# Moving the low halves of the layer norm from GpSimd to VectorE, and issuing the raw-row gathers in one run, in the start-up of a graph network kernel

## The reference

```python
# block 1: graph layer, one LSTM step, projection
xn  = (x - mean(x)) / sqrt(var(x) + 1e-5)            # by row
agg = segment_sum(xn[src], dst, num_segments=6250)
h   = relu(agg @ W_rel + b_rel + xn @ W_root)        # 256 -> 512
i, f, g, o = split(h @ W_ih.T + b_ih + b_hh, 4)      # 512 -> 2048
x   = x + (sigmoid(o) * tanh(sigmoid(i) * tanh(g))) @ W_fc + b_fc
# block 2: slice attention over all rows (8 heads, 64 slices) on layernorm(x)
x   = x + ffn(layernorm(x))
```

## Time and profile before

| what | value |
|---|---|
| median of three runs | 1594.67 us |
| range of the runs | 1590.57 to 1596.51 us |
| span of the profiled execution, first to last instruction | 1292.3 us |
| median less span (launch and end, not in the trace) | 302.4 us |
| busy share: TensorE, VectorE, ScalarE, GpSimd | 92%, 64%, 48%, 65% |
| chain that ended last: TensorE, ScalarE, VectorE | 80%, 10%, 4% |
| granted TensorE clock, mean | 0.995 of 2.4 GHz |

### The profile page before, as it was taken

One profiled execution on the slowest core, in us unless ns is written; L12 is line 12 of the kernel. 1 busy time (PEld: TensorE's weight loads), 2 busy tenths in 40 slices (PEclk: granted clock), 3 DMA queues, 4 the chain that ended last, 5 costly groups with the idle time before them and its releaser, 6 DMA issues.

```text
span 1292.3 us, 25492 instructions
## 1 busy us (share of the span) xinstructions
PE 1182.8 (92%) x8463; PEld 1052.9 (81%) x8463; DVE 830.3 (64%) x2412; ACT 622.6 (48%) x1248; POOL 844.0 (65%) x884
## 2 busy tenths in 40 slices
PE   0317999999999999999999999999999999999998
PEld 0315888898889888888888888888888888897798
DVE  7767375667566756676567656765676667546655
ACT  5662354545454445544554455444544453555332
POOL 4767777777777777777777777777777777600000
PEclk9998999999999999999999999999999999999999
DMA  8674445544554455444544454445544544423499
GB/s 300 206 260 113 121 114 146 143 139 115 144 145 138 123 136 144 137 124 131 144 138 131 127 145 139 135 121 147 142 130 122 146 143 130 114 67 96 124 330 285
DMA packets 122534, 191.82 MB, mean 148 GB/s; under 512 B 51451, under 2 KB 84193, under 8 KB 122457
## 3 DMA queue, kind: packets, MB, share of 16 engines
q0 software_dynamic: 41008, 111.77, 30.1%
q1 hardware_dynamic: 70894, 60.20, 15.8%
q10 hardware_dynamic: 10575, 19.20, 4.4%
HBM read 159.02 MB, written 32.92 MB: 149 GB/s over the span
## 4 chain that ended last, share of the span: by engine, by line
PE 80%; ACT 10%; issue 4%; DVE 4%; DMA 1%; POOL 1%; ACTq 0%; DVEq 0%; SPq 0%; POOLq 0%
PE ps L384 19%; PE ps L386 19%; PE ps L385 19%; PE ps L1039 13%; PE ps L1147 5%; ACT ps L820 3%; ACT L802 2%; ACT x L810 2%; PE ps L1135 2%; PE ps L1099 1%; PE ps L1073 1%; PE ps L1076 1%; ACT ring L753 1%; DVE stats L1346 1%; DMA table<-pick_room 1%
## 5 line engine op out<-in xcount | busy, mean ns | idle before, releaser
L675 POOL DMA_INDIRECT ring<-table,sidx x833 | 797.7, 958 | 258.0 <-issue 251.4
L384 PE MATMUL ps<-h_h,wih_h 128*128 128x256 f32 x1200 | 346.4, 289 | 4.1 <-DVE wxs_l L1666 4.1
L385 PE MATMUL ps<-h_l,wih_h 128*128 128x256 f32 x1200 | 339.8, 283 | 0.0
L386 PE MATMUL ps<-h_h,wih_l 128*128 128x256 f32 x1200 | 339.7, 283 | 0.0
L1039 PE MATMUL ps<-ring,oneh 128*125 128x512 f16 x974 | 229.6, 382 | 26.3 <-DVE oneh L1492 26.3
L384 PEld LDWEIGHTS ps<-h_h,wih_h 128*128 128x128 f32 x1200 | 230.2, 192 | 7.6 <-issue 4.5
L385 PEld LDWEIGHTS ps<-h_l,wih_h 128*128 128x128 f32 x1200 | 230.3, 192 | 1.7
L386 PEld LDWEIGHTS ps<-h_h,wih_l 128*128 128x128 f32 x1200 | 230.2, 192 | 0.0
L835 ACT ACTIVATE gate<-ps,bgate 128x256 f32<-128x256 f32 x300 | 125.8, 472 | 210.6 <-PE ps L386 210.6
L1039 PEld LDWEIGHTS ps<-ring,oneh 128*125 128x125 f16 x974 | 132.3, 138 | 91.8 <-DVE oneh L1492 26.5
L1492 DVE TENSOR_SCALAR oneh<-iota,rel 128x125 f16<-128x125 f16 x974 | 166.4, 286 | 1.8
(11 more groups left out here) (226 smaller groups left out, 2529.9 us busy)
## 6 DMA issues: line engine op xcount, KB each, us to landing
ring<-table,sidx POOLq DMA_INDIRECT x833, 2.7
swt_d<-swt ACTq DMA_DIRECT2D x25, 500.0 KB, 3.0
gate<-swt_d SPq DMA_DIRECT2D x19, 500.0 KB, 6.2
x_room<-in_x SPq DMA_DIRECT2D x12, 512.0 KB, 5.8
xn<-table SPq DMA_DIRECT2D x25, 224.0 KB
xin<-in_x SPq DMA_DIRECT2D x25, 224.0 KB
res<-xin SPq DMA_DIRECT2D x25, 224.0 KB
table<-tile_room SPq DMA_DIRECT2D x8, 512.0 KB, 5.5
```

What stands on the lines that cost most here:

```text
L384: eng.matmul(dst, wh, xh, start=first, stop=False)
L385: eng.matmul(dst, wh, xl, start=False, stop=False)
L386: return eng.matmul(dst, wl, xh, start=False, stop=last)
L675: pool.indirect_dma_start(ring[:, j, :], None, table, bass.IndirectOffsetOnAxis(ap=sidx[:, odd * SLOTS + j:odd * SLOTS + j + 1], axis=0)). ...
```

## The change

VectorE now does the low halves of all 13 chunks: in round k of its first pass, after the statistics of chunk k+2 and the planning step, it does that of chunk k-1. GpSimd does no low half any more. After the wait for the edge lists it issues `gather_x` 0 to 8, then waits for the plan's value and issues the planning gather, then `gather_x` 9 to 17.

```diff
             pool.wait_ge(idx_in[0], LIST)
-            for k in range(NCH - 1):
-                if k == 5:
+            for j in range(RAW):
+                if j == RAW // 2:
                     pool.wait_ge(plan_v, 3)
                     pool.indirect_dma_start(edge_i[0:NW + 1, 0:ER], None, a["dst"].rearrange("(p b) -> p b", b=ER),
                                             bass.IndirectOffsetOnAxis(ap=coli[0:NW + 1, 0:1], axis=0)).then_inc(ld_rows, 16)
-                ln_low(pool, k)
-                if k >= 5:
-                    gather_x(k - 5)
-            for j in range(NCH - 6, RAW):
                 gather_x(j)
             pool.wait_ge(plan_done, 2)
...
                 for n, step in ((2, plan_a), (3, plan_a2), (4, plan_a3), (5, plan_b), (9, bias_rows), (10, plan_c), (11, plan_c2)):
                     if k == n:
                         step()
-            ln_low(dve, NCH - 1)
+                if k:
+                    ln_low(dve, k - 1)
             ln_low(dve, NCH)
             plan_d()
```

## The result

The changed kernel takes 1568.91 us in the median of five runs (1566.51 to 1581.27). Five runs of the kernel before beside them have a median of 1594.67 us (1582.1 to 1596.51).

The account below looks back on a forecast made before the run. It took TensorE and GpSimd's gather stream as both full, the later one deciding: 7.7 us gained on TensorE's path, 6.8 on the stream. Against the median of 1594.67 us, the 6.8 gave 1587.9 us; range 1583.5 to 1595 us.

Parts of the forecast that it names:

- The 302.4 us around the span stay: Whole execution: 302.4 us of the time lie outside the profiled span of 1292.3 us and do not change.
- First pass: Start-up on VectorE: 12.7 us of added low halves, paid by waits and held-up instructions; last store 1.6 us earlier, at 55.5.
- the five held-up instructions: First pass on VectorE: five instructions lengthened beside GpSimd's low halves return to clean durations, giving back 7.7 us.
- Second pass: Start-up on VectorE: 6.6 us of waits for gathered rows go, 0.5 returns; line 1435 starts 7.7 us earlier, at 77.3.
- From there to the first turn nothing changes: Between line 1435 and TensorE's first turn: the 7.7 us gain reaches TensorE's first sums whole.
- GpSimd's stream: Table gathers after the start-up: pair 1 waits for its edge lists, in at 89.8, so the stream starts 6.8 us earlier.
- both engines are full: Main loop: TensorE's turn of 42.86 us equals 34 gather intervals, 42.88 us, on GpSimd; the later engine sets the end.
- rival A: TensorE's path decides, as lists come early enough or the stream has room: gain 7.7 to 9.5 us, chance 0.28.
- Sum: Whole kernel: TensorE's path gains 7.7 us, GpSimd's stream 6.8; the later decides, giving 1587.9 us.
- Rival C: Main-loop gathers lengthen beside VectorE, 0.013 us per interval, 10.6 us in all: slower, 1598.5 us, chance 0.10.
- Rival D: First pass: gathers hold VectorE's fast instructions as subtractions did, last store up to 6.1 us later: 1595.5 us, chance 0.05.
- The rule weighed: Start-up: the skill says GpSimd and fast-mode VectorE instructions exclude each other; the sum let gathers hold up nothing on VectorE.

Follow-up runs that it names:

- e0: The kernel before, unchanged, run again: 1592.49 us, ratio 1.0014 to before.
- e10: The kernel after plus 15 unneeded gathers of raw rows, and VectorE's waits for them, behind the raw gathers on GpSimd: 1591.43 us, ratio 1.0018 to before.
- e1: The kernel after, unchanged, run again: 1571.36 us, ratio 0.9872 to before.
- e9: The kernel before, with GpSimd's table gathers made to wait for the third piece of the second pass: 1583.75 us, ratio 0.9954 to before.
- e8: The kernel after without the gathers of pair 4 and later and the waits for them (result incomplete): 1333.08 us, ratio 0.8378 to before.
- e13: The kernel after with 80 already fulfilled waits ahead of each half of a pair's gathers, from pair 1 on: 1644.64 us, ratio 1.0309 to before.
- e2: The kernel before with all low halves on VectorE, raw gathers kept nearly at their old times: 1594.36 us, ratio 1.0001 to before.
- e7: The kernel after with gathers from pair 4 on fetching 16 rows instead of 128 (result incomplete): 1611.63 us, ratio 1.0146 to before.

## Why the prediction was wrong

**The step that failed** is "The 302.4 us around the span stay". It took the profiled execution of before (span 1292.3) for one of the timed ones and put the difference outside it. With that the sum had no term for the late hand-overs of the ordinary executions, 17.6 us in e0's second pass, which are most of what the change takes away. In every profiled execution after it the span is some 2 us below the time (1582.9 and 1584.72 in e0), and in none of them, of either kernel, does a turn with all gathers take less than 53.8 us. The profiled one ran at 42.86 us a turn and a clock of 0.995, and would have taken about 1294 us (an estimate: its span and the 1.9 us of the others); no run of before, 1575 to 1606 us in all, was like it. A difference of 19% between a profile and its median was the sign, and I explained it away in half a sentence.

**First pass.** Right. Last store issued at 55.33 (forecast 55.5); the five held-up instructions came back; no wait for a chunk or a gather; the wait for ScalarE's high half is 0.7 us (0.8).

**Second pass.** The waits for gathers went as forecast, and were about as large in e0 (4.9 us) as in before's profile (6.6). The term that was missing is the lateness beside a long run of gathers, 17.6 us in e0, nothing in before's profile. The change takes it away because the 18 raw gathers are over by 44.4 us and GpSimd is then silent for 18.5 us; e10 fills the silence and loses the whole gain. "From there to the first turn nothing changes" failed too: the one-hot matrices of after come apart 20 us into the table gathers, and 2.8 us of the gain are lost between line 1431 and the first sums.

**GpSimd's stream.** The reading "both engines are full" holds only in the profiled execution. Ordinarily GpSimd waits a fifth of the main loop (141.8 + 63.8 + 61.1 us and smaller waits of 1385), and the stream is no bound. Its start at 91.22 is released by TensorE's first half window, not by the lists, whose loads are issued from 86.11 and 87.23. So of the cases the mechanism of rival A came true (TensorE's path decides), with more than twice its gain. That the time fell as forecast owes something to luck: the start-up that the sum reckoned with is not the one that was timed.

**Sum.** Forecast 7.7 us on TensorE's path; by e0 and e1 the first sums move 20.3 us and the medians 21.1 us. Rival C, 0.013 us more between gathers, has no place in a stream that waits. Rival D did not happen.

**The rule weighed.** The `ln_row` at 22.80 takes 0.61 us, the one at 14.60 takes 0.41, both while a gather runs: a stretch of 0.2 us at most. The gather at 33.19 takes 1.84 us beside a low half of VectorE. The Trainium skill ("SBUF — State Buffer", Who interferes with whom) has the whole VectorE instruction excluded and, by inference, the gather untouched; for these durations the measurement says otherwise. The one-hots of e9 keep their 0.26 us and only start late, and before's profile, with the same gathers, has none of it.

## What to carry to other kernels

Hold the span of the profiled execution against the times before reading anything else: if they are 300 us apart, profile the unchanged kernel again, since the bound that you read may be that of an execution nobody times. In this kernel a long run of indirect gathers on GpSimd was not free for the others even when no one waited for its rows. Moving it away from the chain of short, dependent instructions helped, and that is worth a trial elsewhere. Test such a suspicion by adding useless gathers (e10) and by leaving out the real ones (e8).

## What the runs showed of the hardware

- Beside a long run of gathers instructions of other engines start late. A wait on a semaphore ends some 3 to 6 us late, also where an engine waits for its own previous instruction (6.44 us at line 1361 of e10). It shows on VectorE and ScalarE, and TensorE pays for it (4.86 us at line 1069 of e1).
- Instructions in plain sequence, which wait for nothing, come late as well, by 0.3 to 2 us: VectorE's one-hots (e9, and at the end of after's start-up) and TensorE's matmuls (13.5 us in 23 gaps in 840 us of e1, 88.7 us in 121 gaps in e13, none in e8).
- The start-up showed it first after 13 us of gathers in e2 and 21 in e0; after's pass, which ends 13.7 us into the table gathers, has none, but neither has the first pass of e10 in 31.7 us of gathers without a gap. So the length of the run is not the whole condition. In the main loop it is there although GpSimd pauses 2 to 3 us at a time. With 16 rows in a gather instead of 128 it did not get less (e7).
- Its price in this kernel is 11.3 us of a turn of 54 us, 238 us in all by e1 and e8, which still gathers for the first four pairs.
- Open: what holds the instructions back. That plain sequences come late too speaks against a matter of the semaphores alone; whether the engines got their next instructions late was not tested, and in e0 the instruction queues moved nothing from 76 to 104 us, where most of the lateness lies. Open too: why one execution, the profiled one of before, had all its gathers and none of the lateness. No run here tells.
